# Keys and queries of a talking-heads attention dealt over 48 partitions, with padded rows in DRAM and a new order of steps

## What is computed

```
def _L0_attn_ref(x, Wqkv, bqkv, Wpre, Wpost, Wout, bout):
    ...
    q = apply_rope(q)
    k = apply_rope(k)
    logits = jnp.einsum('bhid,bhjd->bhij', q, k) * SCALE
    logits = jnp.einsum('bhij,gh->bgij', logits, Wpre)
    attn = jax.nn.softmax(logits, axis=-1)
    attn = jnp.einsum('bhij,gh->bgij', attn, Wpost)
    out = jnp.einsum('bhij,bhjd->bhid', attn, v)
    ...
    return out @ Wout.T + bout

xn = _layernorm(x, axis=-1)
s = _L0_attn_ref(xn, ...)
g = _silu(_L0_ffn_ref(xn, ...))     # 2 layers: qkv, rotary, local attention (window 128), norm, gelu feed-forward
x = x + s * g
```

## Time and profile before

| | us |
|---|---|
| median of the three runs | 5326.17 |
| lowest, highest | 5326.14, 5334.16 |
| the profiled execution's own time | 5316.89 |
| its span, first to last instruction | 5315.1 |
| PE busy | 4465.5 (84%) |
| ACT busy | 3383.7 (64%) |
| DVE busy | 3144.1 (59%) |
| POOL busy | 1769.9 (33%) |
| DMA traffic | 997.59 MB, mean 188 GB/s |

### The profile page before, as it was taken

How to read it: one execution, slowest core, us unless ns; L and a number is a source line. 1 busy time by engine, 2 the same in 40 slices (tenths; PEclk the granted TensorE clock), 3 DMA queues, 4 the chain that set the end, 5 groups by cost and what they waited for, 6 DMA issues and landing times. The chain is left out here.

```text
span 5315.1 us, 184653 instructions
## 1 busy us (share of the span) xinstructions
PE 4465.5 (84%) x75160; PEld 3333.2 (63%) x75160; DVE 3144.1 (59%) x8220; ACT 3383.7 (64%) x8621; POOL 1769.9 (33%) x1069
## 2 busy tenths in 40 slices
PE   3888988888888888888889888888888889888887
PEld 2666666666666666666666666666666666566665
DVE  3556646565566656646566466655666656466654
ACT  2666667666666666666666666665666666666665
POOL 2232333333324332333333333332233423334222
PEclk6899999999999999999999999999999999999999
DMA  6556556555566565555555565555655555565552
GB/s 195 187 187 220 196 177 207 176 190 183 184 210 195 192 180 208 185 176 211 168 203 197 177 208 180 188 190 177 206 192 190 187 205 184 179 210 172 201 169 64
DMA packets 369492, 997.59 MB, mean 188 GB/s; under 512 B 34576, under 2 KB 101136, under 8 KB 350224
## 3 DMA queue, kind: packets, MB, share of 16 engines
q1 hardware_dynamic: 357856, 969.01, 53.8%
q0 software_dynamic: 10800, 16.78, 1.7%
HBM read 655.35 MB, written 338.69 MB: 187 GB/s over the span
## 5 line engine op out<-in xcount | busy, mean ns | idle before, releaser
L1236 ACT ACTIVATE probs<-bank_S,neg_max 128x512 f32<-128x512 f32 x1024 | 692.4, 681 | 584.8 <-DVE neg_max L1488 550.6
L1789 POOL TENSOR_TENSOR l_probs<-l_probs,l_inv 128x1024 f32<-128x1024 f32 (+1 forms) x256 | 429.3, 1680 | 1145.9 <-DVE l_inv L1595 1145.9
L937 PEld LDWEIGHTS bank_M<-mixer_n,probs 64*64 64x64 f32 x32768 | 597.1, 144 | 283.1 <-issue 259.1
L1488 DVE TENSOR_REDUCE neg_max<-bank_S 128x1 f32<-128x512 f32 x1024 | 657.6, 683 | 195.8 <-PE bank_S L920 186.3
L937 PE MATMUL bank_M<-mixer_n,probs 64*64 64x64 f32 x32768 | 655.7, 231 | 125.1 <-issue 102.3
L1774 POOL TENSOR_TENSOR inv_norms<-norms_c,minus_half 128x16 f32<-128x16 f32 x128 | 413.5, 3230 | 896.1 <-DVE norms_c L1529 896.1
L920 PE MATMUL bank_S<-raw_mix,w_pre 64*64 64x512 f32 x4096 | 598.5, 643 | 92.2 <-ACT probs L1236 45.0
L1222 ACT ACTIVATE raw_sb<-bank_S 128x512 f32<-128x512 f32 x1024 | 555.7, 598 | 149.9 <-PE bank_S L906 145.7
L1301 ACT ACTIVATE l_probs<-l_probs,l_least 128x256 f32<-128x256 f32 (+1 forms) x1024 | 480.3, 472 | 114.0 <-DVE l_least L1575 110.7
L1795 POOL TENSOR_TENSOR hidden_lo<-shared,hidden_hi 128x512 fp32r<-128x512 f32 x192 | 244.2, 1287 | 880.2 <-ACT hidden_hi L1372 880.2
L585 DVE COPY mixed<-bank_M 128x512 f32<-128x512 f32 x512 | 351.1, 686 | 310.6 <-PE bank_M L937 308.1
(11 more groups left out here) (161 smaller groups left out, 10270.8 us busy)
## 6 DMA issues: line engine op xcount, KB each, us to landing
raw_all<-raw_sb SPq DMA_DIRECT2D x512, 512.0 KB, 3.3
raw_mix<-raw_all SPq DMA_DIRECT2D x512, 512.0 KB, 4.4
w_qkv_lo<-split_qkv SPq DMA_DIRECT2D x30, 1536.0 KB, 7.9
w_qkv_hi<-split_qkv SPq DMA_DIRECT2D x30, 1536.0 KB, 9.4
w_hi<-split SPq DMA_DIRECT2D x30, 1408.0 KB, 6.2
w_lo<-split SPq DMA_DIRECT2D x30, 1408.0 KB, 7.2
queries<-spilled_q SPq DMA_DIRECT2D x384, 64.0 KB
keys<-spilled_k SPq DMA_DIRECT2D x96, 256.0 KB, 10.5
```

Source lines behind the costliest of these rows:

```text
L937: last = mm(bank[f"M{r}"][keys, at:at + GH * HI], probs[rows, (2 * m + t) % PB, j * P + keys.start:j * P + keys.stop], mixer_n[rows, m % 2 ...
L1236: fn(probs[:, n % PB, :], bank[k][:], ACT.Exp, bias=neg_max[:, n % 2:n % 2 + 1], accum_out=row_sum[:, n % 4:n % 4 + 1]).then_inc(emptied[k ...
L1488: v.tensor_reduce(neg_max[:, t:t + 1], bank[k][:], AX.X, ALU.max, negate=True)\
L1789: g.tensor_tensor(l_probs[:, u % LB, :, lo:], l_probs[:, u % LB, :, lo:], l_inv[:, u % 2, :, None].to_broadcast([P, 4, 2 * P - lo]), ALU.m ...
```

## The change

It has three parts.

1. The DRAM tensors `spilled_q` and `spilled_k` get rows of 528 instead of 512 floats (`ROW_PAD = 16`, 64 bytes); the last 16 are never used. A row of one head feature is then no longer next to the following one, so that what a partition receives in a load of keys (16 KB) is eight pieces of 2 KB in DRAM instead of one.
2. A load of keys or queries went to 16 partitions side by side (`at : at + 16`). It now goes to every third of 48 partitions (`at : at + 48 : 3`). The three parts lie interleaved instead of one after the other, for keys and queries alike, so the matmul over 48 partitions sums the same products.
3. All three orders are new texts. The steps are the same ones.

```
+ROW_PAD = 16
...
-        spilled_q, spilled_k = (nc.dram_tensor(f"spilled_{name}", (2, HP, 2, HALF, HC8, N), F32, kind="Internal").ap()
+        spilled_q, spilled_k = (nc.dram_tensor(f"spilled_{name}", (2, HP, 2, HALF, HC8, N + ROW_PAD), F32, kind="Internal").ap()[:, :, :, :, :, 0:N]
...
                     for i, part in enumerate((0, 0, 1)):
-                        at = hp * SEEN + i * GD
-                        sp.dma_start(keys[at:at + GD].bitcast(F32), spilled_k[part, hp].rearrange("s d c j -> (s d) c j"))\
+                        at = hp * SEEN + i
+                        sp.dma_start(keys[at:at + STACK:3].bitcast(F32), spilled_k[part, hp].rearrange("s d c j -> (s d) c j"))\
...
-                        at = hp * SEEN + i * GD
+                        at = hp * SEEN + i
                         rows = spilled_q[part, hp].rearrange("s d c j -> (s d) c j")
-                        sp.dma_start(queries[at:at + GD].bitcast(F32), rows[:, :, n * P:(n + 1) * P])\
+                        sp.dma_start(queries[at:at + STACK:3].bitcast(F32), rows[:, :, n * P:(n + 1) * P])\
...
 ORDER = """
-scores.0 qkv.0.0 raw.1.0 join.0.0 raw.1.1 mixers.0 bound qkv.0.1 join.0.1 k_turn.0.0 raw.1.2 q_turn.0.0 raw.1.3
+scores.0 qkv.0.0 raw.1.0 join.0.0 mixers.0 qkv.0.1 raw.1.1 bound q_turn.0.0 k_turn.0.0 scores.1 join.0.1 qkv.0.2
```

More of the change, by code:

```diff
@@ new lines @@
+mixers.22 local_values.1.2 split_q p_turn.1.3 mixers.23 scores.24 mix.22 p_turn.1.4 local_values.1.3 mixers.24
+local_scores.1.6 scores.25 mix.23 out_proj.1.1 local_scores.1.7 local_values.1.4 weigh.1.6 p_turn.1.5 values.5
+mixers.25 scores.26 mix.24 raw.0.0 local_values.1.5 raw.0.1 p_turn.1.6 raw.0.2 mixers.26 out_proj.1.2 weigh.1.7
+raw.0.3 mix.25 scores.27 mix.26 local_values.1.6 raw.0.4 p_turn.1.7 raw.0.5 local_values.1.7 scores.28 out_proj.1.3
+mixers.27 half_turn.1 mixers.28 project.2 shift_turn.1 mix.27 raw.0.6 raw.0.7 values.6 h_scale.1 scores.29 h_turn.1
@@ L181 @@
+raw.0.3 mix.25 scores.27 mix.26 local_values.1.6 raw.0.4 p_turn.1.7 raw.0.5 local_values.1.7 scores.28 out_proj.1.3
+mixers.27 half_turn.1 mixers.28 project.2 shift_turn.1 mix.27 raw.0.6 raw.0.7 values.6 h_scale.1 scores.29 h_turn.1
+scores.30 mixers.29 mixers.30 mix.28 up.1.0 up.1.1 mix.29 hide.1.0 hide.1.1 scores.31 up.1.2 up.1.3 hide.1.2 mix.30
+mixers.31 hide.1.3 up.1.4 up.1.5 mix.31 talk_v hide.1.5 hide.1.4 values.7 down.1.0 project.3 down.1.1 down.1.2
+down.1.3
 """
 LAST_ORDER = """
-scores.0 qkv.0.0 raw.1.0 join.0.0 raw.1.1 mixers.0 bound qkv.0.1 join.0.1 k_turn.0.0 raw.1.2 q_turn.0.0 raw.1.3
@@ L205 @@
-out_proj.1.2 p_turn.1.6 mixers.26 local_values.1.6 p_turn.1.7 mix.25 scores.27 mix.26 local_values.1.7 scores.28
-mixers.27 out_proj.1.3 half_turn.1 shift_turn.1 mix.27 mixers.28 scores.29 values.6 mixers.29 h_scale.1 mix.28
-h_turn.1 mix.29 scores.30 mixers.30 up.1.0 up.1.1 hide.1.0 hide.1.1 scores.31 up.1.2 mix.30 up.1.3 hide.1.2 mixers.31
-hide.1.3 up.1.4 mix.31 up.1.5 values.7 project.3 down.1.0 down.1.1 down.1.2 hide.1.5 down.1.3 hide.1.4 end.bound
-end.sigmoid.0 end.sigmoid.1 end.sigmoid.2 end.sigmoid.3 end.silu end.gated end.store
+scores.0 qkv.0.0 raw.1.0 join.0.0 mixers.0 qkv.0.1 raw.1.1 bound q_turn.0.0 k_turn.0.0 scores.1 join.0.1 qkv.0.2
@@ new lines @@
+local_values.1.5 p_turn.1.6 mixers.26 out_proj.1.2 weigh.1.7 mix.25 scores.27 mix.26 local_values.1.6 p_turn.1.7
+local_values.1.7 scores.28 out_proj.1.3 mixers.27 half_turn.1 mixers.28 project.2 shift_turn.1 mix.27 values.6
+h_scale.1 scores.29 h_turn.1 scores.30 mixers.29 mixers.30 mix.28 up.1.0 up.1.1 mix.29 hide.1.0 hide.1.1 scores.31
+up.1.2 up.1.3 hide.1.2 mix.30 mixers.31 hide.1.3 up.1.4 up.1.5 mix.31 hide.1.5 hide.1.4 values.7 down.1.0 project.3
+down.1.1 down.1.2 down.1.3 end.bound end.sigmoid.0 end.sigmoid.1 end.sigmoid.2 end.sigmoid.3 end.silu end.gated
@@ L210 @@
+end.store
 """
```

136 lines of the change are left out of this document (63 added, 73 removed).

## The result

The changed kernel took **5347.16 us** (median of 8 runs, 5334.94 to 5353.13); the kernel before took 5324.82 beside it (8 runs, 5309.74 to 5336.56). The ratio is 1.0043 with a 95% interval of 1.0026 to 1.0060: the change makes the kernel 0.4% slower. I had predicted 5248 and a faster kernel. The profiled execution took 5334.9 us, its span is 5333.1 us, the mean granted clock 0.939 (before 0.944).

A forecast was written before the change was run, and what follows sets the result against it. PE's work plus some 850 us idle bounds the kernel, with PE's instructions late behind the keys' loads. On the profiled 5316.9 us, -65 -15 -5 +15 = -70 gives 5247, taken as 5248; range 5145 to 5330, the forecast's own 5200 to 5295.

The forecast's parts named there:

- The keys' stall, -65: In the 15 stretches after the keys' issue, PE gets back 65 us of 94.7 us idle, its instructions coming late.
- 11.0 to 6 us: Transfer of a batch's six keys loads: 11.0 us at 143 GB/s before, taken as 6 us over 48 partitions.
- second rival: "Nothing gets faster" (5310 us), chance 0.14: engine or DRAM, not where the data lands, slows the keys' loads.
- First batch, -5: PE's wait for the first keys, covered by nothing: a shorter transfer saves 5 us, bounds 0 and 8.
- Clock, -15: PE's half-speed clock around the keys' stall: 1 us per batch comes back, 15 us, bounds 0 and 30.
- Order on PE, +15: New order of PE's steps: new pairs of `raw` steps and `h_turn.0` cost 15 us, 1 a batch.
- Order on SP, 0: Loads of `raw_mix` for `scores.25` go out behind the keys, some 7.5 us later, but just in time: price 0.
- Queries, 0: The 384 loads of queries: PE waits for them in no row; 0 to -15 us, taken as 0.
- padding, nothing: 64 bytes of padding a row in DRAM: by a Trainium skill page it does nothing, the partitions do all.
- Slower (5365): Rival, chance 0.16: at `scores.25` PE waits up to 6 us per batch for `raw_mix` behind the keys; 5365 us.
- nothing gets faster: Rival, chance 0.14: the keys' loads stay at 143 GB/s, the stall moves, only the order counts; 5310 us.

The follow-up runs named there:

- e1: Kernel before, in its old orders, with the change's loads over 48 partitions and padded rows: 5299.9 us, ratio 0.9952.
- e2: Changed kernel keeping its three new orders, but with unpadded rows and loads on 16 adjacent partitions as before: 5368.3 us, ratio 1.0076.
- e13: Only 256 KB loads, no kernel, singly and six in flight: six took 15.2 us on 16 adjacent partitions, 13.4 us on every third of 48.
- e3: Kernel before, old orders and unpadded rows, with only the loads dealt over 48 partitions: 5292.4 us, ratio 0.9932.
- e4: Kernel before, old orders and 16 adjacent partitions, with only the rows padded: 5326.2 us, ratio 0.9998.
- e8: Kernel before, each keys load after the first batch cut from 256 KB to 8 KB, output not the reference's: 5202.6 us, ratio 0.9766.
- e5: Changed kernel with the step `keys` moved back behind `scores.23`, so two `raw_mix` loads go out ahead of the keys: 5375.9 us, ratio 1.0090.
- e15: Changed kernel without the row padding (new orders, 48 partitions): 5344.7 us, ratio 1.0030.
- e7: Kernel before with loads on 48 partitions, `values.5` moved behind `p_turn.1.5` and `project.2` behind `half_turn.1`: 5315.1 us, ratio 0.9974.
- e6: Changed kernel with four `raw` steps moved, so none stand side by side except where they did before: 5423.4 us, ratio 1.0185.
- e16: Kernel before with loads on 48 partitions, the new order only in steps 270 to 281, and `values.5` five steps later: 5252.1 us, ratio 0.9861.
- e17: Changed kernel with `scores.12` moved behind `mix.10` and `scores.13` behind `mix.11`, so ACT loads its function table 97 times, not 129: 5340.8 us, ratio 1.0025.
- e18: e16 with `mix.29` and `scores.31` moved ahead of `up.1.0`, for 65 ACT table loads instead of 97: 5317.6 us, ratio 0.9981.

## Why the prediction was wrong, step by step

The step that failed most is the gain from the loads: the terms -65, -15 and -5 came to 27 us (e1) and not 85, because the transfer of the keys hardly got shorter. The second is the order's +15, which measured +41 (e2). The mechanism behind the first, a transfer that keeps PE's instructions from coming, held.

- **The keys' stall, -65.** Failed by size, at the step "11.0 to 6 us". The transfer got 1.8 us shorter (e13: 15.2 to 13.4 for six), not 5, and PE got back 9.4 us of its busy time in the stretches (e3), not 65. The pieces of 2 KB, which I had thought would let others in, did nothing (e4). That the transfer starves PE of instructions held in full: without it 121 us go (e8). I had inferred the rate from the number of partitions alone, although the first load, by itself and as slow, stood in the earlier trace rows and I had named it as the second rival's evidence.
- **First batch, -5.** The wait for the first keys fell from 53.1 to 50.6 us, -2.5. In the range.
- **Clock, -15.** Failed by sign: matmuls took 45.0 us more. I had priced the clock only where a stall went, and not where waits came. In the rows above, waits of 2.22 and 5.52 us that the new order puts ahead of a step are followed by matmuls at half speed, and steps behind its new waits take longer over the batches: `scores.2` 17.4 to 28.6, `mix.2` 30.6 to 45.3, `mix.10` 18.6 to 29.5 us.
- **Order on PE, +15 (bounds -75 to +75).** +41 (e2), within its bounds. Two of its parts were near: the second steps of the new `raw` pairs wait 1.3 to 2.3 us each and `raw.1.1` no longer waits, so that all `raw` steps but `raw.0.0` went only from 164.7 to 189.5 us. One was wrong: `h_turn.0` waits 0 and not more than 2.86, as its cover stood ahead of it. The largest part was not in my list at all: new waits ahead of `scores.23`, `scores.30`, `mix.19`, `k_turn.0.0` and `local_values.1.6`, 15 to 19 us each over the batches, 25.8 us ahead of `raw.0.0` for ACT's `probs`, and the slower matmuls.
- **Order on SP, 0.** `scores.25` does wait for `raw_mix`, 35.7 us over the batches where I wrote "it just fits". In batch 7 both sides of that sum are off: the load lands 11.1 us after its issue (2628.73), with the keys ahead of it, not 4.4; and PE has 5.6 us of work left, not 9, since `values.5`, which I counted as cover, now stands behind `scores.25`. Along with this wait, the stall of `values.5` (87.6 to 3.8 us) went. e5 shows that the two are one: take the wait away and the stall is back. As a term of its own it is worth less than nothing.
- **Queries, 0; padding, nothing.** Held: PE waits 0.2 us for queries after; e4 0.9998, e15 beside after. That the queries are not far away shows in e7, where PE waits 78.8 us for them.
- **The rivals.** "Slower (5365)" had the direction and the right place and wait, but not the cause, by e5. The nearest in mechanism was "nothing gets faster": the place of the data sets the rate far less than I took, and then the order counts. It had +15 for the order; with +41 and -27 it would have given 5331 on the profiled 5317, and the profiled execution after took 5335.

What stays open: what sets the rate of six loads in flight, 12% apart where one load alone gets its packets through 19% sooner; why instruction packets still come late for most of the 182 us of idle time inside steps that e8 leaves; and which rule makes an order of steps good. The sections' exchange shows only that it isn't a sum over places.

## What to carry to other kernels

Before a transfer is reshaped for its rate, take it away once (e8) to see what it costs, and time the old and the new shape alone (e13): the two runs bound the gain from both sides. An idle time that the profile names is worth its length only if nothing else is late at that place: of six edits that each removed a named wait, stall or table load (e5, e6, e7, e16, e17, e18), four lost 26 to 78 us, e17 gained less than the intervals tell, and only e16 gained some 28 us, at their edge. And price a wait of some us on PE with the slow matmuls behind it, not by its length alone.

## What the hardware showed

- PE's instructions come through the same DMA engines as the data, and where these are full, behind the loads of the keys before, PE stands 2.8 to 9.1 us inside `values.5` in 14 of 15 batches with nothing to wait for. The Trainium skill (Runtime: NRT & Kernel Launch, "Instruction fetch mechanics") has blocks of 16 KiB, 256 instructions, fetched ahead by DMA at a cost "mostly hidden". The size agrees with 9.90 MB in 604 packets; the cost does not: one transfer of 1.57 MB a batch makes the kernel 121 us slower (e8).
- A load of 256 KB to 16 partitions side by side or to every third of 48: 15.2 and 13.4 us for six in flight. The Trainium skill (SBUF — State Buffer, "Door 1: The DMA port swizzle") gives the second twice the first's rate, by the ports reached. The direction agrees, the factor of two does not appear: 12% in flight, and alone a round trip of 4.1 and 4.0 us. One load alone moves its packets at about 136 GB/s side by side and 168 by threes (256 KB from first packet to last). So the 143 GB/s of my prediction are not above the rule's 109 because several loads are in flight; one load alone is above it too.
- Loads to partitions three apart also take SP longer to issue: six take 3.8 us in most batches after and 2.7 before (2.74 in the earlier trace rows; the 4.73 in SP's row above and the 3.88 of the earlier trace rows are both on the long side).
